# Expert routing after attention: sixteen small rankings inside the key-block loop, or one ranking over all blocks behind it

## What is computed

```python
x = x + LN(attention(LN(x)))     # weights = softmax(q k^T / 32); out[k] = sum over q of weights[q,k] v[q]
x = x + LN(ffn(LN(x)))

# ffn on xt (tokens x 1024)
scores  = softmax(xt @ gate_w.T)                 # 16 experts
g       = scores.reshape(T, 4, 4)                # 4 groups of 4
keep the 2 groups with the greatest maximum, others to 0
c       = scores of the 4 greatest that are left, 0 elsewhere     # T x 16
y       = sum over e of c[:, e] * ((silu(xt @ w1[e]) * (xt @ w3[e])) @ w2[e])
z       = (silu(xt @ ws1) * (xt @ ws3)) @ ws2
out     = y + z
```

## Time and profile before

| | us |
|---|---|
| median of 2 runs | 6304.04 |
| the two runs | 5925.8, 6682.28 |
| the profiled execution | 5925.48 |
| its span on the slowest core (core 7) | 5924.0 |
| spans of the eight cores | 5898.8 to 5924.0 |

### The profile page before, as it was taken

How to read it: one execution, slowest core, us unless ns; L and a number is a source line. 1 busy time by engine, 2 the same in 40 slices (tenths; PEclk the granted TensorE clock), 3 DMA queues, 4 the chain that set the end, 5 groups by cost and what they waited for, 6 DMA issues and landing times.

```text
span 5924.0 us, 57494 instructions; the slowest of 8 cores (5898.8 to 5924.0 us)
## 1 busy us (share of the span) xinstructions
PE 4151.6 (70%) x18864; PEld 1934.8 (33%) x18864; DVE 2253.7 (38%) x4876; ACT 1133.0 (19%) x1484; POOL 205.7 (3%) x117
## 2 busy tenths in 40 slices
PE   4685322239999999999346852232399999999992
PEld 3232111114444444444122321111244444444440
DVE  2223444433333333333522234444333333333335
ACT  2232111121111111111132321111211111111111
POOL 0000000000000000000000000000000000000000
PEclk7787555559999999999667875655699999999996
DMA  3000000031122122110230000000321221122103
GB/s 107 29 8 14 22 22 22 22 114 66 63 86 78 59 78 86 63 66 33 96 121 29 8 15 22 22 22 22 114 77 59 79 86 64 65 86 75 64 23 110
DMA packets 125320, 339.32 MB, mean 57 GB/s; under 512 B 6228, under 2 KB 6228, under 8 KB 125032
## 3 DMA queue, kind: packets, MB, share of 16 engines
q1 hardware_dynamic: 125032, 335.65, 16.3%
HBM read 302.07 MB, written 33.55 MB: 57 GB/s over the span
## 4 chain that ended last, share of the span: by engine, by line
PE 64%; DVE 15%; issue 7%; ACT 6%; DMA 5%; DVEq 1%; ACTq 0%; SPq 0%
PE PS L33 64%; DVE st L33 4%; DVE sc_sm L33 4%; DVE sgt L33 3%; ACT RK L33 2%; DMA RK<-x 2%; DVE RK L33 2%; ACT L33 1%; DVEq L57 1%; DVE RA L33 1%; DMA RV<-w 1%; DVE RV L33 1%; ACT RA L33 1%; ACT RV L33 1%; DMA RA<-Wq 1%
## 5 line engine op out<-in xcount | busy, mean ns | idle before, releaser
L33 PE MATMUL PS<-RQ,RW 128*128 128x512 bf16 x9216 | 2039.5, 382 | 158.8 <-ACT RK L33 103.9
L33 PEld LDWEIGHTS PS<-RQ,RW 128*128 128x128 bf16 x9216 | 905.8, 99 | 1273.8 <-issue 210.3
L33 DVE SCALAR_TENSOR_TENSOR RA<-PS,c_buf,RA 128x1024 f32<-128x1024 f32 x480 | 616.0, 1283 | 1119.9 <-PE PS L33 1119.4
L33 PE MATMUL PS<-RW,RK 128*128 128x512 bf16 x4608 | 1023.9, 379 | 3.9 <-DVE RK L33 2.7
L33 PE MATMUL PS<-identf,RK 128*128 128x128 f32 x256 | 62.1, 424 | 1019.3 <-ACT RK L33 1019.3
L33 ACT ACTIVATE RK<-PS 128x512 f32<-128x512 f32 x576 | 332.5, 597 | 1794.5 <-PE PS L33 1794.5
L33 DVE TENSOR_TENSOR RK<-RK,PS 128x512 bf16<-128x512 f32 x576 | 396.1, 688 | 667.8 <-PE PS L33 667.8
L33 PEld LDWEIGHTS PS<-RW,RK 128*128 128x128 bf16 x4608 | 431.3, 97 | 573.3 <-issue 96.3
L33 POOL CAST RW<-RV 128x2048 bf16<-128x2048 f32 x108 | 204.5, 1893 | 5441.4 <-DMA RV<-w 2863.6
L33 PEld LDWEIGHTS PS<-identf,RK 128*128 128x128 f32 x256 | 50.2, 223 | 1034.1 <-issue 1034.1
L33 ACT CAST RW<-RV 128x2048 bf16<-128x2048 f32 x108 | 204.8, 1897 | 809.9 <-PE PS L33 748.0
(11 more groups left out here) (66 smaller groups left out, 1876.5 us busy)
## 6 DMA issues: line engine op xcount, KB each, us to landing
RV<-w SPq DMA_DIRECT2D x192, 1024.0 KB, 6.9
RV<-ws SPq DMA_DIRECT2D x24, 1024.0 KB, 6.6
RA<-x SPq DMA_DIRECT2D x32, 512.0 KB, 3.9
RK<-x SPq DMA_DIRECT2D x32, 512.0 KB, 3.9
x1park<-RK SPq DMA_DIRECT2D x32, 512.0 KB, 2.6
RK<-x1park SPq DMA_DIRECT2D x32, 512.0 KB, 4.2
out<-RV SPq DMA_DIRECT2D x32, 512.0 KB, 2.9
RA<-Wq SPq DMA_DIRECT2D x4, 2048.0 KB, 12.9
```

The source lines that it names most:

```text
L33: self._last = getattr(self.e, name)(*a, **k)
```

## The change

The row max and the Exp of each round go. ScalarE copies each round's 16 logits from PSUM to a new tile `glog` of 128 x (16 rounds x 16 experts). Behind the loop, once per sequence, ScalarE takes one Exp over the 256 columns (no maximum is subtracted), and VectorE does the softmax division and both rankings for all 16 blocks at once in 81 instructions, on 3-D views (block, expert) of up to 240 columns. `f_t` waits for this. In `emit_ln` a mark is renamed: `v1` is now set one instruction earlier, and the Sqrt waits for the new name `vs` where `v1` was. The tiles `sgt` and `sc_sm` go; `glog`, `smkb`, `gsc` come.

```diff
-        sgt = ent(nc.sbuf_tensor("sgt", [P, 48], F32))
-        sc_sm = ent(nc.sbuf_tensor("sc_sm", [P, 3 * NEXP + 8], F32))
         den = ent(nc.sbuf_tensor("den", [P, 2 * QB], F32))
         c_buf = ent(nc.sbuf_tensor("c_buf", [P, TT * NEXP], F32))
+        glog = ent(nc.sbuf_tensor("glog", [P, QB * NEXP], F32))
+        smkb = ent(nc.sbuf_tensor("smkb", [P, QB * NEXP], F32))
+        gsc = ent(nc.sbuf_tensor("gsc", [P, 10 * QB], F32))
...
@@ -228,14 +229,15 @@
                 v.scalar_tensor_tensor(out=sq_ap, in0=src_ap, scalar=negm,
                                        in1=src_ap, op0=ALU.add, op1=ALU.mult,
                                        accum_out=veps)
-                v.wait(v.mark())
+                mput(key + "v1", v.mark())
+                v.wait(mget(key + "v1"))
                 v.tensor_scalar(out=veps, in0=veps, scalar1=1.0 / D, scalar2=EPS,
                                 op0=ALU.mult, op1=ALU.add)
-                mput(key + "v1", v.mark())
+                mput(key + "vs", v.mark())
             pr.on("v", vb)
 
             def sb(s):
-                s.wait(mget(key + "v1"))
+                s.wait(mget(key + "vs"))
                 s.activation(rstd, veps, AF.Sqrt)
                 mput(key + "sq", s.mark())
             pr.on("s", sb)
@@ -708,90 +710,103 @@
                         mput(f"b{b}k{kb}gmm", t.mark())
                     pr.on("t", a3_t3)
 
-                    def a3_gv(v, b=b, kb=kb):
+                    def a3_gl(s, b=b, kb=kb):
                         gb = 6 + kb % 2
-                        v.wait(mget(f"b{b}k{kb}gmm"))
-                        v.wait(mget(f"b{b}k{kb - 1}glog"))
-                        v.reduce_max(sgt[:, 0:1], bank(gb)[:, 0:NEXP], axis=AX.X,
-                                     negate=True)
-                        mput(f"b{b}k{kb}gmax", v.mark())
-                    pr.on("v", a3_gv)
-
-                    def a3_gs(s, b=b, kb=kb):
-                        gb = 6 + kb % 2
-                        s.wait(mget(f"b{b}k{kb}gmax"))
-                        s.wait(mget(f"b{b}k{kb - 1}cdone"))
-                        s.activation(sc_sm[:, 0:NEXP], bank(gb)[:, 0:NEXP], AF.Exp,
-                                     bias=sgt[:, 0:1], scale=1.0, accum_out=sgt[:, 1:2])
+                        s.wait(mget(f"b{b}k{kb}gmm"))
+                        if kb == 0 and b > 0:
+                            s.wait(mget(f"b{b - 1}gatedone"))
+                        s.copy(glog[:, kb * NEXP:(kb + 1) * NEXP],
+                               bank(gb)[:, 0:NEXP])
                         mput(f"b{b}k{kb}glog", s.mark())
-                    pr.on("s", a3_gs)
-
-                    def a3_gv2(v, b=b, kb=kb):
-                        E = NEXP
-                        sco = sc_sm[:, 0:E]
-                        smk = sc_sm[:, E:2 * E]
-                        cnt = sc_sm[:, 2 * E:3 * E]
-                        gmx = sc_sm[:, 3 * E:3 * E + 4]
-                        gcnt = sc_sm[:, 3 * E + 4:3 * E + 8]
-                        v.wait(mget(f"b{b}k{kb}glog"))
-                        v.reciprocal(sgt[:, 2:3], sgt[:, 1:2])
-                        v.wait(v.mark())
-                        v.tensor_scalar(out=sco, in0=sco, scalar1=sgt[:, 2:3],
-                                        scalar2=None, op0=ALU.mult)
-                        v.wait(v.mark())
...
-                        for sh in range(1, 4):
-                            for piece in range(2):
-                                if piece == 0:
...
-                        for sh in range(1, E):
-                            for piece in range(2):
-                                if piece == 0:
-                                    w = E - sh
-                                    a_ap, b_ap, o_ap = smk[:, sh:E], smk[:, 0:w], cnt[:, 0:w]
-                                else:
-                                    w = sh
-                                    a_ap, b_ap, o_ap = smk[:, 0:sh], smk[:, E - sh:E], cnt[:, E - sh:E]
-                                tmp = sgt[:, 32:32 + w]
-                                v.tensor_tensor(out=tmp, in0=a_ap, in1=b_ap, op=ALU.is_gt)
-                                v.wait(v.mark())
-                                if sh == 1:
-                                    v.tensor_copy(o_ap, tmp)
-                                else:
-                                    v.tensor_tensor(out=o_ap, in0=o_ap, in1=tmp, op=ALU.add)
-                                v.wait(v.mark())
-                        v.tensor_scalar(out=cnt, in0=cnt, scalar1=3.5, scalar2=None,
-                                        op0=ALU.is_le)
-                        v.wait(v.mark())
-                        if kb == 0 and b > 0:
-                            v.wait(mget(f"b{b - 1}ffn_v_done"))
-                        v.tensor_tensor(out=c_buf[:, kb * E:(kb + 1) * E], in0=smk,
-                                        in1=cnt, op=ALU.mult)
-                        mput(f"b{b}k{kb}cdone", v.mark())
-                    pr.on("v", a3_gv2)
+                    pr.on("s", a3_gl)
+                def gate_s(s, b=b):
+                    s.wait(mget(f"b{b}k{QB - 1}glog"))
+                    s.activation(glog[:], glog[:], AF.Exp)
+                    mput(f"b{b}gexp", s.mark())
+                pr.on("s", gate_s)
+
+                def gate_v(v, b=b):
+                    E = NEXP
+                    KB = QB
+                    gmax = gsc[:, 0:4 * KB]
+                    den16 = gsc[:, 4 * KB:5 * KB]
+                    gcnt = smkb[:, 0:4 * KB]
+                    gtmp = gsc[:, 5 * KB:9 * KB]
+                    v.wait(mget(f"b{b}gexp"))
+                    if b > 0:
+                        v.wait(mget(f"b{b - 1}ffn_v_done"))
+                    g3 = glog[:].rearrange("p (k e) -> p k e", k=KB)
+                    v.tensor_reduce(out=den16, in_=g3, axis=AX.X, op=ALU.add)
+                    v.wait(v.mark())
+                    v.reciprocal(den16, den16)
+                    v.wait(v.mark())
+                    v.tensor_tensor(out=g3, in0=g3,
+                                    in1=den16.rearrange("p (k o) -> p k o", o=1
+                                                        ).to_broadcast([P, KB, E]),
+                                    op=ALU.mult)
+                    v.wait(v.mark())
+                    v.tensor_reduce(out=gmax,
+                                    in_=glog[:].rearrange("p (kg c) -> p kg c", c=4),
+                                    axis=AX.X, op=ALU.max)
+                    v.wait(v.mark())
...
+                    for sh in range(1, 4):
+                        for piece in range(2):
+                            if piece == 0:
+                                w = 4 - sh
+                                a_ap, b_ap = gm3[:, :, sh:4], gm3[:, :, 0:w]
+                                o_ap, t_ap = gc3[:, :, 0:w], gt3[:, :, 0:w]
+                            else:
+                                w = sh
+                                a_ap, b_ap = gm3[:, :, 0:sh], gm3[:, :, 4 - sh:4]
+                                o_ap, t_ap = gc3[:, :, 4 - sh:4], gt3[:, :, 4 - sh:4]
+                            v.tensor_tensor(out=t_ap, in0=a_ap, in1=b_ap, op=ALU.is_gt)
+                            v.wait(v.mark())
+                            if sh == 1:
+                                v.tensor_copy(o_ap, t_ap)
+                            else:
+                                v.tensor_tensor(out=o_ap, in0=o_ap, in1=t_ap, op=ALU.add)
+                            v.wait(v.mark())
+                    v.tensor_scalar(out=gcnt, in0=gcnt, scalar1=1.5, scalar2=None,
+                                    op0=ALU.is_le)
+                    v.wait(v.mark())
+                    v.tensor_copy(gtmp[:, 0:4 * KB], gcnt)
+                    v.wait(v.mark())
+                    v.tensor_tensor(out=smkb[:].rearrange("p (kg c) -> p kg c", c=4),
+                                    in0=glog[:].rearrange("p (kg c) -> p kg c", c=4),
+                                    in1=gtmp[:, 0:4 * KB].rearrange("p (kg o) -> p kg o", o=1
+                                                                    ).to_broadcast([P, 4 * KB, 4]),
+                                    op=ALU.mult)
+                    v.wait(v.mark())
...
+                    for sh in range(1, E):
+                        for piece in range(2):
+                            if piece == 0:
+                                w = E - sh
+                                a_ap, b_ap = s3[:, :, sh:E], s3[:, :, 0:w]
+                                o_ap, t_ap = c3[:, :, 0:w], t3[:, :, 0:w]
+                            else:
+                                w = sh
+                                a_ap, b_ap = s3[:, :, 0:sh], s3[:, :, E - sh:E]
+                                o_ap, t_ap = c3[:, :, E - sh:E], t3[:, :, E - sh:E]
+                            v.tensor_tensor(out=t_ap, in0=a_ap, in1=b_ap, op=ALU.is_gt)
+                            v.wait(v.mark())
```

(14 more changed lines are left out.)

31 lines of the change are left out of this document (6 added, 25 removed).

## The result

The change makes the kernel faster. The ratio after to before is 0.921, with a 95% interval of 0.918 to 0.924. The medians over all executions are 6098.35 us before (10 runs, 5919.44 to 6682.28) and 5665.7 us after (11 runs, 5459.14 to 6173.13). In many executions of either kernel the four cores of one die (0 to 3 or 4 to 7) are granted a lower TensorE clock than the others and end later, which the two medians include, while the ratio and all spans from here on are of executions or dies without it.

A forecast was written before the change was run, and what follows sets the result against it. The prediction took attention's second half to be bound by a ring of waits, with routing arithmetic delaying the layernorm: 5925.5 - 446 (gaps and table loads) + 0 (tail) = 5480 us, range 5440 to 5535.

The follow-up runs named there:

- `st` of 600: The kernel before with the small tile `st` of 600 instead of 32 columns, moving the tiles behind it; median span 5920.0 us, kernel before 5910.4 and 5919.4.

## What to carry to other kernels

In a stage where no engine is full, look for the instruction that is ready but queued behind unrelated work of its own engine, and price that gap, not the busy time of the work: 80 instructions of 0.17 us cost 13.7 us a round because they stood in front of a layernorm, and the one batch of 36 us that does their work cost nothing behind the loop, where the weights were late. After such a stall is gone the next one may again be a matter of queue order: here three more moves (two of order, one of a load's own tile) took 509 us, where the first took 457. When the times that you are given lie far apart, make the number and the range for the figure that will be reported.

## What was not expected of the hardware

- The load of 512 KB of x from DRAM in A3 takes in the median 3.6 to 3.7 us (even cores; 3.9 on two of them in the kernel with `st` of 600) or 3.9 to 4.0 (odd) in kernels with 4876 VectorE instructions, and 3.2 to 3.4 us in those with 2366 to 3084; with 4750, 3.4 to 3.5 on all cores. Issued early it takes 4.0 to 4.1 us also with 2478. The cause is open.
- Switching ScalarE's table costs the 1.28 us of its load and no more (VectorE's wait for the Sqrt grew from 0.40 to 1.68), and nothing where it lies beside other work.
- A two-input VectorE instruction that starts while a GpSimd cast of 1.9 us runs ends only with it (1.74 us for 80 columns, where the like instruction behind it took 0.24); one that had started 0.1 us before the cast took its usual 0.34. The Trainium skill ("SBUF — State Buffer", Who interferes with whom) describes the port that both share as a lock held for the whole instruction, and the trace agrees.
